# Retention layer: four tiles in step in a loop, loads in the order of their use; last layer: the block buffers cleared by ScalarE

## The reference

```
def msr(x, Wq, Wk, Wv, Wg, Wo, gg, gb, D):
    q, k = (x @ Wq).reshape(b, s, 8, 32), (x @ Wk).reshape(b, s, 8, 32)
    v = (x @ Wv).reshape(b, s, 8, 32)
    scores = jnp.einsum('bnhd,bmhd->bhnm', q, k) * D      # D: causal decay, one per head
    y = jnp.einsum('bhnm,bmhd->bnhd', scores, v).reshape(b, s, H)
    y = group_norm(y, gg, gb)                             # per head
    return jax.nn.silu(x @ Wg) * y @ Wo
for i in range(2):                                        # two sublayers
    xn = layer_norm(x, ln_gamma, ln_beta)
    ret = msr(xn, Wq[i], Wk[i], Wv[i], Wg[i], Wo[i], gn_gamma[i], gn_beta[i], D) + x
    rn = layer_norm(ret, ln_gamma, ln_beta)
    ffn = jax.nn.gelu(rn @ W1[i] + b1[i]) @ W2[i] + b2[i]
    x = ffn + ret
```

## Time and profile before

| | us |
|---|---|
| median of 3 runs | 4538.15 |
| lowest and highest run | 4524.79, 4539.03 |
| the profiled execution | 4520.55 |
| its span | 4518.7 |

### The profile page before, as it was taken

The page is one execution under the profiler, slowest core; times in us unless marked ns, Lnnn a source line. Parts: engine busy times, 40 slices in busy tenths (PEclk is TensorE's granted clock), DMA queues, the critical chain, the costliest instruction groups (busy, mean ns, idle before and its releaser), DMA issues. The chain is left out here.

```text
span 4518.7 us, 69708 instructions
## 1 busy us (share of the span) xinstructions
PE 3612.0 (80%) x26668; PEld 2573.3 (57%) x26672; DVE 2635.7 (58%) x5422; ACT 1766.7 (39%) x3341; POOL 358.6 (8%) x566
## 2 busy tenths in 40 slices
PE   7999999987768887826888669788888876885777
PEld 5555657876755564613565535455555555664666
DVE  6889884442567878765444462367767653443443
ACT  4888881112353443412323112244444422322333
POOL 3000000000000000000111000011111101110000
PEclk8556559998876666657988789899999988988788
DMA  2000001000010000010000121000000002000000
GB/s 76 1 0 0 0 0 70 0 8 11 12 49 1 0 0 0 0 57 5 7 3 7 57 56 74 2 3 3 3 3 5 3 1 113 1 1 1 1 1 10
DMA packets 43830, 72.80 MB, mean 16 GB/s; under 512 B 25693, under 2 KB 33377, under 8 KB 40293
## 3 DMA queue, kind: packets, MB, share of 16 engines
q1 hardware_dynamic: 35432, 70.54, 4.4%
q10 hardware_dynamic: 8256, 0.52, 0.2%
HBM read 67.91 MB, written 3.15 MB: 16 GB/s over the span
## 5 line engine op out<-in xcount | busy, mean ns | idle before, releaser
L1316 DVE TENSOR_SCALAR_CACHE_REDUCE l0x_ex<-l0x_s_ps 128x1024 f32<-128x1024 f32 x258 | 305.6, 1222 | 56.5 <-PE l0x_s_ps L1019 55.6
L1151 ACT ACTIVATE l0x_ex<-l0x_ex,l0x_neg_max,l0x_q_scale 128x2048 f32<-128x2048 f32 x128 | 268.0, 2094 | 51.8 <-DVE l0x_neg_max L1322 50.0
L1019 PE MATMUL l0x_s_ps<-l0x_kT,l0x_qT 64*128 64x512 bf16 x516 | 231.8, 591 | 34.0 <-ACT l0x_qT L1146 19.9
L1031 PEld LDWEIGHTS l0x_t_ps<-l0x_identb,l0x_pb 128*128 128x128 bf16 x2048 | 196.8, 141 | 109.0 <-issue 53.2
L1158 ACT ACTIVATE l0x_pt<-l0x_t_ps 128x1024 bf16<-128x1024 bf16 x256 | 246.1, 1013 | 26.2 <-PE l0x_t_ps L1031 25.9
L1031 PE MATMUL l0x_t_ps<-l0x_identb,l0x_pb 128*128 128x128 bf16 x2048 | 230.5, 301 | 7.7 <-ACT l0x_pt L1158 4.0
L1331 DVE TENSOR_SCALAR l0x_pb<-l0x_ex 128x2048 bf16<-128x2048 f32 x128 | 156.3, 1222 | 0.0
L263 PE MATMUL l3x_bank<-l3x_wproj,l3x_cat 128*128 128x256 f32 x512 | 121.3, 391 | 32.2 <-DVE l3x_cat L3345 32.2
L263 PE MATMUL l3x_bank<-l3x_w_kv_x,l3x_ctxT 128*128 128x512 f32 x256 | 130.5, 658 | 0.9 <-ACT l3x_ctx_q L762 0.9
L263 PEld LDWEIGHTS l3x_bank<-l3x_wproj,l3x_cat 128*128 128x128 f32 x512 | 96.5, 193 | 52.6 <-DVE l3x_cat L3345 38.7
L840 ACT ACTIVATE l3x_e<-l3x_e 128x1024 f32<-128x1024 f32 x24 | 25.4, 1057 | 250.4 <-DVE l3x_e L860 250.4
(11 more groups left out here) (741 smaller groups left out, 8697.7 us busy)
## 6 DMA issues: line engine op xcount, KB each, us to landing
l3x_wproj<-in_L_xattn_wproj SPq DMA_DIRECT2D x1, 4096.0 KB, 25.4
l3a_w<-in_L_attn_W SPq DMA_DIRECT2D x2, 2048.0 KB, 12.6
l2f_w<-in_L_ffn_w SPq DMA_DIRECT2D x1, 2816.0 KB, 11.6
l0x_ctxT<-in_ctxT SPq DMA_DIRECT2D x8, 256.0 KB, 2.9
l0a_wq<-in_L_attn_W_Q SPq DMA_DIRECT2D x1, 2048.0 KB
l0a_wk<-in_L_attn_W_K SPq DMA_DIRECT2D x1, 2048.0 KB
l0a_wv<-in_L_attn_W_V SPq DMA_DIRECT2D x1, 2048.0 KB, 7.9
l0a_wo<-in_L_attn_W_O SPq DMA_DIRECT2D x1, 2048.0 KB, 13.3
```

The source lines that it names most:

```text
L1019: ins = mm(s_ps[:, j * 512:(j + 1) * 512], qT[rows, h // 2, :], kT[rows, h // 2, j * 512:(j + 1) * 512], start=True, stop=True)
L1031: ins = nc.tensor.transpose(t_ps[:, j * P:(j + 1) * P], pb[:, h % 2, j * P:(j + 1) * P], identb[:])
L1151: s.activation(ex[:, h % 4, :], ex[:, h % 4, :], ACT.Exp, scale=q_scale[:, h:h + 1], bias=nb[:, h:h + 1], accum_out=sums[:, h:h + 1]).then ...
L1316: v.tensor_scalar(ex[:, h % 4, c], s_ps[:, c], 1.0, None, ALU.mult, ALU.max, accum_out=mx[:, h, half:half + 1]).then_inc(o.up(scores_taken ...
```

## The change

In the retention layer the delay between the tiles goes: all four programs step together, and the two generations become a hardware loop of two passes on each engine (`Fori`), with six `yield`s fewer. SyncE issues six small loads and `own` first, then the first sublayer's halves of q, k, v, g and o (with the decay mask behind k), its w1 and w2, and then the second sublayer's halves. VectorE starts the norms with no wait for loads and waits for the eight loads of `L.dma_in` before it spreads q; ScalarE waits for these eight at its start; PE waits for them and the five first halves ahead of the first q projection, and for the second halves in the second sublayer. In the last layer ScalarE clears the four block buffers, by a copy of a broadcast 128x128 tensor with scale 0, and VectorE sets the two small ones only.

```diff
@@ -3739,6 +3739,7 @@
         ln_g, ln_b = L.sb("ln_gamma", [P, DC]), L.sb("ln_beta", [P, DC])
         decay, own = L.sb("decay", [P, H, P]), L.sb("own", [P, 4])
         bank = L.banks(8)
+        small = 8
         by_head = lambda a: a[:].rearrange("p (h e) -> p h e", e=HD)
         wide = lambda a: a[:].unsqueeze(2).broadcast_to([P, H, HD])
 
@@ -3767,6 +3768,8 @@
                     yield from inner.tensor(pe, t, act_bank, 2 * l + 1)
                     yield
                     pe.wait_ge(inner.ready.sem, inner.ready.value(t, 2 * l + 1))
+                    pe.wait_ge(L.dma_in, 16 * small)
+                    pe.wait_ge(*((second_loaded, 16 * 7) if l else (first_loaded, 16 * 5)))
                     for n, ps in (("q", dve_bank), ("k", act_bank)):
                         for m in range(DC):
                             project(nc, ps[:, m * P:(m + 1) * P], lambda c: w[n][:, l, c, m * P:(m + 1) * P], lambda c: xT[:, c, :], DC)
@@ -3795,7 +3798,7 @@
                     yield from inner.tensor(pe, t, act_bank, 2 * l + 2)
                     yield
                     pe.wait_ge(inner.ready.sem, inner.ready.value(t, 2 * l + 2))
-                    pe.wait_ge(L.dma_late, 16 * L.late_loads)
+                    pe.wait_ge(L.dma_late, 16 * 2)
                     for m in range(FC):
                         ins = project(nc, bank[m // 4][:, (m % 4) * P:(m % 4 + 1) * P], lambda c: w1[:, l, c, m * P:(m + 1) * P], lambda c: xT[:, c, :], DC)
                     ins.then_inc(hid_ps.sem, 1)
@@ -3803,7 +3806,6 @@
                     pe.wait_ge(hid_ready.sem, hid_ready.value(t, k))
                     nc.tensor.matmul(dve_bank[:, 0:D], env.ones_row[:, 0:P], b2[:, l * D:(l + 1) * D], start=True, stop=False)
                     project(nc, dve_bank[:, 0:D], lambda c: hid[:, c, :], lambda c: w2[:, l, c, :], FC, start=False).then_inc(ffn_ps.sem, 1)
-                yield
 
             def scalar_program(act, t):
                 s = nc.scalar
@@ -3844,12 +3844,11 @@
                     pool.wait_ge(have_var.sem, have_var.value(t, l + 1))
                     nc.gpsimd.tensor_tensor(rstd[:], var[:], env.neg_half[:].broadcast_to([P, H]), ALU.pow).then_inc(o.up(have_rstd), 1)
                     pool.wait_ge(have_rstd.sem, o.at(have_rstd))
-                    yield from steps(2)
+                    yield
                     yield from inner.pool(o, 2 * l + 2)
                     yield from steps(2)
                 pool.wait_ge(o.sem, o.at())
                 pool.sem_inc(o.sem, o.rest())
-                yield
 
             def vector_program(dve, t):
                 v = nc.vector
@@ -3861,6 +3860,7 @@
                     src = norm.y if l == 0 else cur
                     yield from inner.vector(o, src[:], 2 * l + 1)
                     yield
+                    dve.wait_ge(L.dma_in, 16 * small)
                     dve.wait_ge(qkv_ps.sem, qkv_ps.value(t, k))
                     for c in range(DC):
                         v.tensor_tensor(qT[:, 4 * c:4 * c + 4, :], dve_bank[:, c * P:(c + 1) * P].unsqueeze(1).broadcast_to([P, 4, P]),
@@ -3909,52 +3909,54 @@
                 dve.wait_ge(o.sem, o.at())
                 dve.wait_ge(o.sem, o.at())
                 dve.sem_inc(o.sem, o.rest())
-                yield
 
             L.tag = ""
             return {"tensor": tensor_program, "scalar": scalar_program, "gpsimd": gpsimd_program, "vector": vector_program}
 
         tiles = [one_of_four(n, bank[2 * n:2 * n + 2]) for n in range(WAYS)]
+        first_loaded, second_loaded = L.sem("first_sublayer_loaded"), L.sem("second_sublayer_loaded")
         block = L.block()
-
-        def in_its_turn(n, program, eng):
-            yield from steps(n * 5 // 2)
-            for t in range(TILES // WAYS):
-                yield from program(eng, t)
 
         @block.sync
         def _(sp):
             d = env.dram
+            for dst, name in ((ln_g, "ln_gamma"), (ln_b, "ln_beta"), (b1, "b1"), (b2, "b2"), (gn_g, "gn_gamma"), (gn_b, "gn_beta")):
+                sp.dma_start(dst[:], d["L3_attn_" + name]).then_inc(L.dma_in, L.loaded())
+            sp.dma_start(own[:], d["own32"]).then_inc(L.dma_in, L.loaded())
             for n in "qkvgo":
-                sp.dma_start(w[n][:], d["L3_attn_W" + n]).then_inc(L.dma_in, L.loaded())
-            for dst, name in ((b1, "b1"), (b2, "b2"), (gn_g, "gn_gamma"), (gn_b, "gn_beta"), (ln_g, "ln_gamma"), (ln_b, "ln_beta")):
-                sp.dma_start(dst[:], d["L3_attn_" + name]).then_inc(L.dma_in, L.loaded())
-            sp.dma_start(decay[:], d["decay"]).then_inc(L.dma_in, L.loaded())
-            sp.dma_start(own[:], d["own32"]).then_inc(L.dma_in, L.loaded())
-            sp.dma_start(w1[:], d["L3_attn_W1"]).then_inc(L.dma_late, L.loaded_late())
-            sp.dma_start(w2[:], d["L3_attn_W2"]).then_inc(L.dma_late, L.loaded_late())
+                sp.dma_start(w[n][:, 0], d["L3_attn_W" + n][:, 0]).then_inc(first_loaded, 16)
+                if n == "k":
+                    sp.dma_start(decay[:], d["decay"]).then_inc(L.dma_in, L.loaded())
+            sp.dma_start(w1[:, 0], d["L3_attn_W1"][:, 0]).then_inc(L.dma_late, L.loaded_late())
+            sp.dma_start(w2[:, 0], d["L3_attn_W2"][:, 0]).then_inc(L.dma_late, L.loaded_late())
+            for n in "qkvgo":
+                sp.dma_start(w[n][:, 1], d["L3_attn_W" + n][:, 1]).then_inc(second_loaded, 16)
+            sp.dma_start(w1[:, 1], d["L3_attn_W1"][:, 1]).then_inc(second_loaded, 16)
+            sp.dma_start(w2[:, 1], d["L3_attn_W2"][:, 1]).then_inc(second_loaded, 16)
             load_next(sp, env)
 
         @block.tensor
         def _(pe):
-            pe.wait_ge(L.dma_in, 16 * L.loads)
-            in_turn(*(in_its_turn(n, tile["tensor"], pe) for n, tile in enumerate(tiles)))
+            with pe.Fori(0, TILES // WAYS) as t:
+                in_turn(*(tile["tensor"](pe, t) for tile in tiles))
 
         @block.scalar
         def _(act):
-            act.wait_ge(L.dma_in, 16 * L.loads)
+            act.wait_ge(L.dma_in, 16 * small)
             s = nc.scalar
-            in_turn(*(in_its_turn(n, tile["scalar"], act) for n, tile in enumerate(tiles)))
+            with act.Fori(0, TILES // WAYS) as t:
+                in_turn(*(tile["scalar"](act, t) for tile in tiles))
 
         @block.gpsimd
         def _(pool):
-            in_turn(*(in_its_turn(n, tile["gpsimd"], pool) for n, tile in enumerate(tiles)))
+            with pool.Fori(0, TILES // WAYS) as t:
+                in_turn(*(tile["gpsimd"](pool, t) for tile in tiles))
 
         @block.vector
         def _(dve):
             v = nc.vector
-            dve.wait_ge(L.dma_in, 16 * L.loads)
-            in_turn(*(in_its_turn(n, tile["vector"], dve) for n, tile in enumerate(tiles)))
+            with dve.Fori(0, TILES // WAYS) as t:
+                in_turn(*(tile["vector"](dve, t) for tile in tiles))
 
 
 def l3_ffn_weights(W):
@@ -4228,7 +4230,7 @@
                     "blocks": pb, "ones": vv[:, :, HD:HV], "shared_weight": cw[:, 0:1]}
 
         tiles = [one_of_four(n, bank[2 * n:2 * n + 2]) for n in range(WAYS)]
-        set_up = L.sig("set_up")
+        set_up, cleared = L.sig("set_up", 2 * WAYS), L.sig("cleared", WAYS)
         block = L.block()
 
         def in_its_turn(n, program, eng):
@@ -4247,6 +4249,9 @@
 
         @block.scalar
         def _(act):
+            for tile in tiles:
+                nc.scalar.activation(tile["blocks"][:], env.ident[:].unsqueeze(1).broadcast_to([P, H, P]), ACT.Copy, scale=0.0).then_inc(cleared.sem, 1)
+            act.wait_ge(cleared.sem, cleared.value())
             act.wait_ge(env.own.sem, env.own.value())
             act.wait_ge(set_up.sem, set_up.value())
             in_turn(*(in_its_turn(n, tile["scalar"], act) for n, tile in enumerate(tiles)))
@@ -4258,13 +4263,9 @@
         @block.vector
         def _(dve):
             v = nc.vector
-            s = Order(dve, L.sem("setup_order"))
             for tile in tiles:
-                v.memset(flat(tile["blocks"][:]), 0.0).then_inc(s.up(), 1)
-                v.memset(tile["ones"], 1.0).then_inc(s.up(), 1)
-                v.memset(tile["shared_weight"], 1.0 / 8.0).then_inc(s.up(), 1)
-            dve.wait_ge(s.sem, s.at())
-            dve.sem_inc(set_up.sem, 1)
+                v.memset(tile["ones"], 1.0).then_inc(set_up.sem, 1)
+                v.memset(tile["shared_weight"], 1.0 / 8.0).then_inc(set_up.sem, 1)
             dve.wait_ge(env.own.sem, env.own.value())
             in_turn(*(in_its_turn(n, tile["vector"], dve) for n, tile in enumerate(tiles)))
 
```

## The result

| | before | after |
|---|---|---|
| median of the runs, us | 4535.27 | 4481.07 |
| lowest and highest of four runs | 4524.79, 4539.03 | 4473.88, 4484.00 |
| profiled execution, its span | 4520.55, 4518.7 | 4482.40, 4480.6 |

A forecast was written before the change was run, and what follows sets the result against it. PE was taken to bound the retention layer, losing 129 of 395 us to idle time and low clock. Gains of 47.6 there and 6.2 in the last layer make 53.8; with the 17.6 to the median carried over, 4484.4 us, range 4466 to 4503.

The forecast's parts named there:

- The steps of the round: Retention layer, four tiles in step, PE's phases and exposed pauses added up: 80.9 us per round, 316.6 for four rounds.
- the generation boundary: Retention layer, both ends included: VectorE's last additions, branch, norm statistics and first normalise no longer covered by neighbouring tiles; 12 us.
- rival 1: Retention layer: each of nine phase changes costs PE 0.7 us more, 25 us in all, so 4509 us; chance 0.14.
- The clock term: Retention layer: PE's clock drops in pauses and work behind them runs slow; 15 us plus 9 us charged.
- The 2.5 behind a group norm: Retention layer: slow clock after each of four group-norm pauses, charged 2.5 us apiece.
- the 2.5 at each generation start: Retention layer: slow clock at each of two generation starts, charged 2.5 us apiece.
- The 1.5 per short turn: Retention layer: slow clock after each of six 3.5 us turns between phases, 1.5 us apiece, 9 us in all.
- Rival 3: Retention layer: clock stays low from group norm through feed-forward, 32 us a round, 128 in all, 4612 us; chance 0.06.
- the prediction's sentence on it: On PE's pauses: the Trainium skill says gaps between matmul bursts bring the clock back to half rate; no size given.
- Start and loads: Retention layer's start: VectorE's norms and the reordered loads both end near 3737, first q projection at 3737.6.
- The last layer: Last layer's head: ScalarE clears four buffers in 7.8 us and becomes the late engine; 6.2 us gained.
- Rival 4: Retention layer: GpSimd and VectorE slow each other in step, 12 us a round, 48 in all, 4532 us; chance 0.07.

The follow-up runs named there:

- The kernel with identity matmuls: Changed kernel plus result-neutral 128x128 identity matmuls on PE where it would wait in the retention layer; layer 349.8 us, run median 4468.98, ratio 0.9859.
- the series 408.1, 378.4, 357.5: Retention layer in us, all with the new loads: tiles staggered as before, two pairs five steps apart, all four in step (the changed kernel).
- GpSimd's share: Against the kernel with identity matmuls: fewer of these, GpSimd multiplies SiLU(g) by gamma and beta, VectorE does three operations; layer 356.6 us, ratio 0.9863.

## Why the prediction was right

**The steps of the round.** They hold. From phase start to phase start at full clock: q, k, v 10.6 (11.0 forecast), scores 6.9 (7.5), gate and mixing with the pause 20.7 (20.9), hidden projection 14.4 (14.3), feed-forward with its turn 20.6 (20.2). Only the output projection with its turn is 8.2 where 7.0 was forecast: VectorE adds and takes the statistics of all four tiles, 1.24 apart, before it normalises the first. A round is 81.4 against 80.9, the generation boundary 12.4 from its first idle to q against 12, of which the loop's 0.9 (0.7 forecast). No gap shows at the changes of phase without a norm, which was rival 1's claim.

**The clock term was mis-sized.** I charged 24 us, and the layer came out 8.9 under the forecast (357.46 against 413.94 - 47.6 = 366.34). Against the full-clock times, the profiled changed kernel paid 1.2, 1.6, 0.6 and 1.4 in q, k, v; 1.3, 1.5, 1.2 and 1.3 in the output projection until its turn; 0.8 in the transposes ahead of it; 0.6 in three turns and 0.7 in one hidden projection: 12.3. Worked out in the same way, the other two traces of the changed kernel paid about 10 and 14. The 2.5 behind a group norm was too much, because part of the slow batch (1.9 over 3.62 on the average) hides behind VectorE's additions; the 2.5 at each generation start was 1.2 and 0.6. The 1.5 per short turn was paid behind two feed-forward turns only, and almost never behind the output projection, since 0.7 showed there once in four. Less clock (-11.7), a later start (+0.7) and longer rounds (+1.8) make up the 8.9 to 0.3. The kernel with identity matmuls shows the mechanism. Rival 3, a clock that stays low, did not happen: 1.00 from 3807.3 to 3824, and three of the four hidden projections took 14.4.

The Trainium skill ("TensorE: Matmul & The Clock Gate", "Why this matters for your kernels") has PE-idle gaps between bursts bring the clock down. The 10 us pauses agree. But the page speaks of gaps above a certain length, which the prediction's sentence on it leaves out. As a rule for every pause it would have been wrong here: the short turns after the output projection cost 0.7 once in four.

**Start and loads.** 13.2 us to the first q was forecast, 13.9 to 15.8 came in the three traces of the changed kernel. VectorE's chain was right (11.6 to the first transposes, 11.1 forecast); the loads, which I let end at the same time, can end last, through the mask. In the profiled run ScalarE waited 0.2 for it.

**The last layer.** 6.2 forecast; the head itself gained 7.1 (16.8 to 9.8), the whole layer 3.1 in the profiled pair, but 6.0 by the means (381.0 in the three traces with the old clears, 375.0 in nine with the new). ScalarE was the late one as forecast; four clears took 7.31 and not 7.8.

**The whole.** 53.8 forecast, 59.6 in the two touched layers of the profiled pair, 54.2 in the medians. That the profiled execution before lay 17.6 under the median also has its place now: its 3724.4 for the unchanged layers is the lowest of the fourteen traces, whose highest is 3749.0. Carrying that difference over was right. That 4484.4 lies within 3.3 of the median is luck in part, though: the layers gained 5.8 more than forecast, and the median of these few runs happened to show less of it. For the same kernel, beside other runs, the medians differ by 60.5 (4534.12 to 4473.62) and by 54.5 (4533.54 to 4479.02).

**Rival 4.** It failed as well: VectorE's operations stayed at 0.42, as GpSimd does only the small powers there; its contention exists, but it takes two-input work of full tiles on GpSimd to show it. The advice that stood beside it ("Perfetto Trace Analysis", "Optimization Strategy" in the Trainium skill: interleaving such stretches may help) did not pay here, by the series 408.1, 378.4, 357.5.

## What to carry to other kernels

Where one engine is the bound and its work per phase exceeds the answer time of the others, put the tiles in step and count the exposed pauses: a few long ones, priced from rows, can be cheaper than short idle times everywhere, which also cost clock. Look for what a wait holds back beside its purpose: an engine that waits for a load it doesn't use starts late, and a clear at the head of the engine that is late anyway costs its whole length (on VectorE about 8.5 us here), while on an engine with slack it costs the part that sticks out (1.5 on ScalarE). Compare the layers that were touched and not spans of single executions, as the unchanged part alone moved by 25 us here.

## What the runs showed of the hardware

- The unchanged layers took 3724.4 to 3749.0 us in fourteen executions, with a granted clock of 0.57 to 0.60 in their first 680 us; what decides it stayed open.
- A pause of 10 us with four transpose pairs in it leaves the next 16 matmuls at 5.2 to 5.9 us in place of 3.62; a shorter one (two operations less per tile, 6.5 us) left them at 5.3 to 6.2. With identity matmuls in the pause (16 ahead of the first transposes, then 5 per tile) they take 3.62 in all four rounds; in the kernel with 12 and 2 of them and GpSimd's share two of the four rounds showed 5.1.
- A 128x256 multiply on VectorE takes 0.42 us, and 0.83 when it starts while GpSimd multiplies two 128x256 tensors in 0.7 to 0.85. GpSimd's power on 128x8 left it at 0.42.
